# Toeplitz convolution in a recurrent block: eight products instead of ten in each middle block, with paired lags and paired inputs

## The reference, cut to what matters

```python
xn = layernorm(x)                                  # x: 2 x 1024 rows of 512
y = irfft(rfft(xn, n=1024) * rfft(K, n=1024))[..., :512]   # causal convolution along the 512 features
s = y + D[0] * xn                                  # K: 512 taps from a state-space model
h1, h3 = lora_linear(xn, w1), lora_linear(xn, w3)  # 512 -> 1376
g = silu(lora_linear(silu(h1) * h3, w2))           # 1376 -> 512
out = x + s * g
```

## Time and profile before

| what | value |
|---|---|
| median of 3 runs | 409.83 us (409.52 to 410.25) |
| the profiled execution: its time, its span | 409.98 us, 408.2 us |
| granted TensorE clock, mean | 0.999 |
| PE busy | 403.3 us (99% of the span), 1850 matmuls |
| DVE busy | 170.1 us (42%) |
| ACT busy | 105.9 us (26%) |
| POOL busy | 73.3 us (18%) |

### The profile page before, as it was taken

The page is one execution under the profiler, slowest core; times in us unless marked ns, Lnnn a source line. Parts: engine busy times, 40 slices in busy tenths (PEclk is TensorE's granted clock), DMA queues, the critical chain, the costliest instruction groups (busy, mean ns, idle before and its releaser), DMA issues.

```text
span 408.2 us, 5004 instructions
## 1 busy us (share of the span) xinstructions
PE 403.3 (99%) x1850; PEld 335.8 (82%) x1850; DVE 170.1 (42%) x267; ACT 105.9 (26%) x175; POOL 73.3 (18%) x139
## 2 busy tenths in 40 slices
PE   8999999999999999999999999999999999999996
PEld 8988888887788888888888888888888888888885
DVE  5887776794793322232343221233234111211125
ACT  7554232222351111221221111112222111111122
POOL 6685645402500114000000103300000000000000
PEclk9999999999999999999999999999999999999999
DMA  8573755604425101000016101000002000000002
GB/s 269 166 184 108 231 156 152 171 26 90 145 78 180 52 2 51 2 0 0 2 51 205 53 0 52 0 0 0 0 0 103 2 0 0 2 0 0 2 0 103
DMA packets 14466, 26.89 MB, mean 66 GB/s; under 512 B 2768, under 2 KB 4528, under 8 KB 14320
## 3 DMA queue, kind: packets, MB, share of 16 engines
q1 hardware_dynamic: 13440, 24.53, 19.2%
q0 software_dynamic: 720, 1.60, 2.0%
q10 hardware_dynamic: 288, 0.52, 0.3%
HBM read 21.45 MB, written 4.54 MB: 64 GB/s over the span
## 4 chain that ended last, share of the span: by engine, by line
PE 94%; DVE 3%; issue 1%; DMA 1%; ACT 1%; POOL 0%; DVEq 0%; POOLq 0%
PE h L991 20%; PE h L992 20%; PE h L993 20%; PE f L991 10%; PE f L992 10%; PE f L993 10%; PE h L1014 2%; PE spare L978 1%; DMA xn<-x_dram 1%; DVE raw L768 1%; PE spare L993 1%; PE spare L973 1%; PE spare L992 1%; PE spare L991 1%; DVE w L783 0%
## 5 line engine op out<-in xcount | busy, mean ns | idle before, releaser
L991 PE MATMUL h<-xt,w 128*128 (+2 forms) x340 | 131.4, 386 | 0.0
L992 PE MATMUL h<-xt,w 128*128 (+2 forms) x340 | 131.2, 386 | 0.0
L993 PE MATMUL h<-xt,w 128*128 (+2 forms) x340 | 131.2, 386 | 0.0
L991 PEld LDWEIGHTS h<-xt,w 128*128 128x128 f32 x340 | 63.9, 188 | 13.3 <-DVE w L780 0.4
L993 PEld LDWEIGHTS h<-xt,w 128*128 128x128 f32 x340 | 63.9, 188 | 12.9
L992 PEld LDWEIGHTS h<-xt,w 128*128 128x128 f32 x340 | 63.9, 188 | 12.3
L837 DVE TENSOR_TENSOR g<-g,h 128x512 f32<-128x512 f32 x40 | 27.5, 686 | 106.3 <-PE h L993 106.1
L842 DVE TENSOR_TENSOR ghl<-g,ghl 128x512 fp32r<-128x512 f32 x44 | 32.4, 736 | 90.0 <-ACT ghl L668 90.0
L991 PE MATMUL f<-ghl,w2f 128*128 128x512 f32 x176 | 68.8, 391 | 0.0
L992 PE MATMUL f<-ghl,w2f 128*128 128x512 f32 x176 | 68.6, 390 | 0.0
L993 PE MATMUL f<-ghl,w2f 128*128 128x512 f32 x176 | 68.5, 389 | 0.0
(11 more groups left out here) (141 smaller groups left out, 310.4 us busy)
## 6 DMA issues: line engine op xcount, KB each, us to landing
raw<-w_dram SPq DMA_DIRECT2D x28, 256.0 KB, 3.9
xres<-xT_dram SPq DMA_DIRECT2D x4, 1024.0 KB, 6.9
outT_dram<-xres SPq DMA_DIRECT2D x15, 256.0 KB, 2.5
rows_next<-x_dram SPq DMA_DIRECT2D x4, 512.0 KB, 3.6
scale_rows<-scales_scratch SPq DMA_DIRECT2D x3, 512.0 KB, 4.2
rows<-x_dram SPq DMA_DIRECT2D x2, 512.0 KB, 7.1
dft_sb<-dft_dram SPq DMA_DIRECT2D x1, 1024.0 KB, 5.0
raw<-w_dram SPq DMA_DIRECT2D x4, 224.0 KB, 3.2
```

The source lines that it names most:

```text
L991: pe.matmul(out, w[1], m[0], start=start, stop=False)
L992: pe.matmul(out, w[0], m[1], start=False, stop=False)
L993: return pe.matmul(out, w[0], m[0], start=False, stop=stop)
```

## The change

In blocks 1 and 2 the ten Toeplitz products become eight. Three use a sum of two inputs and a sum of two lags: with S(a,b) the product of such a pair, `(T0 + T1)(x0 + x1)` minus `T0 x0` and `T1 x1` gives `T1 x0 + T0 x1`, which is output chunk 1, and so on for the pairs (0, 2) and (1, 2). Blocks 0 and 3 keep their ten products.

- PE: `products` runs five of the eight behind `down` in tiles 2 (two products, T0 x0 and T1 x1, in the two spare banks), 4 (paired), 5 (T2 x2) and 6 (paired), all but the first two in the bank `spare1`. `last_product` runs the last three behind tile 10, and then `down` of tile 10 follows in one piece. The waits of the first gate and up part of a middle or last block become `conv_used` 1 and 2.
- DVE: `pair_sum` (three dependent additions for each pair, in tiles 4, 5 and 7 at "gate"), `pair_low` (the low part of the sum, in the same tiles at "up", behind `hidden_lo`), and `mix` (eight additions, subtractions and copies in all), which combines the products. `mid_sum` does what `out_sum` did.
- ACT: `pair_high` casts the high part of each pair's sum. `mid_gate` is `out_gate` with other buffers. Behind `out_gate` of block 0 ACT casts the high parts of the summed lags once.
- POOL: sums the lags once (T1 + T0 and T2 + T0 in one instruction of 256 columns, T1 + T2 in one of 128), behind `next_scale(1, 1)` of block 0, and subtracts the high parts when ACT has cast them. In the loop its wait for the convolution before `next_scale` is on `conv_used` instead of `conv_ready`.

The diff, without the new constants, addresses and semaphores that say nothing more:

```diff
--- before.py
+++ after.py
@@ -208,6 +208,16 @@
 K_PARTS = D // P
+MIX_AT = {(3, "gate"): (0,), (5, "gate"): (1,), (6, "gate"): (2,), (7, "gate"): (3,)}
+PAIRS = ((0, 1), (0, 2), (1, 2))
+PAIR_AT, PAIR_LO_AT = {(4, "gate"): 0, (5, "gate"): 1, (7, "gate"): 2}, {(4, "up"): 0, (5, "up"): 1, (7, "up"): 2}
+PRODUCTS_AT = {2: ((0, 0), (1, 1)), 4: ((0, 1),), 5: ((2, 2),), 6: ((0, 2),)}
+PRODUCTS = 5
 def spare_uses():
@@ -345,6 +365,12 @@
         gate = at("gate", [P, 2, BLK], lora_off + DC * BLK * 4)
         rows_next = at("rows_next", [P, 2, D], lora_off + (DC + 2) * BLK * 4)
         scale_rows = at("scale_rows", [P, 2, BLK], lora_off + (DC + 4) * BLK * 4)
+        pair_f = at("pair_whole", [P, BLK], lora_off + (DC + 3) * BLK * 4)
+        pair_lo = at("pair_lo", [P, BLK], lora_off + (DC + 3) * BLK * 4, F32R)
+        pair_hi = at("pair_hi", [P, BLK], tz_off, F32R)
+        y1, y2, less = gate[:, 0, :], gate[:, 1, :], rows_next[:, 0, :]
         assert lora_off + (DC + 6) * BLK * 4 <= xn_off
         rows_tile = 9
@@ -690,12 +719,28 @@
                         act.wait_ge(res_done, e - 1)
                     nc.scalar.activation(gate[:, n % 2, :], f[c][:, :], ACT.Silu).then_inc(gate_done, 1)
+            def pair_high(b, k):
+                act.wait_ge(pair_step, 9 * b - 9 + 3 * k + 3)
+                nc.scalar.copy(pair_hi[:, :], pair_f[:, :]).then_inc(pair_cast, 1)
+            def mid_gate(b):
+                for n, c in enumerate(OUT_ORDER):
+                    e = b * DC + n
+                    act.wait_ge(f_ready, e + 1)
+                    act.wait_ge(res_done, e - 1)
+                    nc.scalar.activation(scale_rows[:, n % 2, :], f[c][:, :], ACT.Silu).then_inc(gate_done, 1)
             def body(b, par_next, first, last):
+                mid = not first and not last
                 norm_at = NORM_AT_FIRST if first else NORM_AT
                 for j in range(HT):
                     for place in ("gate", "up", "down"):
                         if place == "gate" and not (first and j == 0):
                             hidden(b, j)
+                        if mid and (j, place) in PAIR_AT:
+                            if PAIR_AT[j, place] == 0:
+                                act.wait_ge(tsum_done, 2)
+                            pair_high(b, PAIR_AT[j, place])
                         if first:
                             for kind, t in folds(place, j):
                                 fold_hi(kind, t)
@@ -723,8 +768,13 @@
                     next_hi(b + 1, c, par_next)
                 if last:
                     last_gate(b)
+                elif mid:
+                    mid_gate(b)
                 else:
                     out_gate(b)
+                    act.wait_ge(tsum_added, 2)
+                    nc.scalar.copy(tsum[:, 0, :, :], tsum_f[:, :, :]).then_inc(tsum_hi, 1)
+                    nc.scalar.copy(t12_hi[:, :], t12_f[:, :]).then_inc(tsum_hi, 1)
             for r in (1, 2):
@@ -849,11 +899,65 @@
                 for i, (n, out, cols) in enumerate(steps):
                     part = gate_last(n)[:, cols]
                     dve.wait_ge(gate_done, b * DC + n + 1)
-                    dve.wait_ge(conv_ready, b * DC + i + 1)
+                    dve.wait_ge(conv_ready, DC + i + 1)
                     nc.vector.tensor_tensor(part, part, out[:, cols], ALU.mult).then_inc(conv_used, 1)
                     dve.wait_ge(conv_used, b * DC + i + 1)
                     sum_ = resid(par, LAST_ORDER[n])[:, cols]
                     nc.vector.tensor_tensor(sum_, sum_, part, ALU.add).then_inc(res_done, 1)
+            def pair_sum(b, par, k):
+                lo, hi = [[xt[:, par, hl, c, :].bitcast(F32) for c in PAIRS[k]] for hl in (1, 0)]
+                n = 9 * b - 9 + 3 * k
+                whole = pair_f[:, :]
+                nc.vector.tensor_tensor(whole, lo[0], lo[1], ALU.add).then_inc(pair_step, 1)
+                dve.wait_ge(pair_step, n + 1)
+                nc.vector.tensor_tensor(whole, whole, hi[0], ALU.add).then_inc(pair_step, 1)
+                dve.wait_ge(pair_step, n + 2)
+                nc.vector.tensor_tensor(whole, whole, hi[1], ALU.add).then_inc(pair_step, 1)
+            def pair_low(b, k):
+                dve.wait_ge(pair_cast, 3 * b - 3 + k + 1)
+                nc.vector.tensor_tensor(pair_lo[:, :], pair_f[:, :], pair_hi[:, :].bitcast(F32), ALU.subtract) \
+                    .then_inc(pair_ready, 1)
+            def mix(b, stage):
+                p, m, s = PRODUCTS * b - PRODUCTS, PRODUCTS * b - PRODUCTS, 3 * b - 3
+                dve.wait_ge(prod_ready, p + stage + 1)
+                if stage == 0:
+                    nc.vector.tensor_copy(y2, sp[1][:, :]).then_inc(mix_step, 1)
+                    dve.wait_ge(mix_step, s + 1)
+                    nc.vector.tensor_tensor(y1, sp[0][:, :], y2, ALU.add).then_inc(mix_done, 1)
+                if stage == 1:
+                    dve.wait_ge(mix_done, m + 1)
+                    nc.vector.tensor_tensor(y1, sp[1][:, :], y1, ALU.subtract).then_inc(mix_done, 1)
+                if stage == 2:
+                    nc.vector.tensor_tensor(less, y2, sp[1][:, :], ALU.add).then_inc(mix_step, 1)
+                    nc.vector.tensor_tensor(y2, y2, sp[1][:, :], ALU.subtract).then_inc(mix_done, 1)
+                    dve.wait_ge(mix_done, m + 3)
+                    nc.vector.tensor_tensor(y2, y2, sp[0][:, :], ALU.subtract).then_inc(mix_step, 1)
+                if stage == 3:
+                    dve.wait_ge(mix_step, s + 3)
+                    nc.vector.tensor_tensor(y2, y2, sp[1][:, :], ALU.add).then_inc(mix_done, 1)
+                if stage == 4:
+                    dve.wait_ge(mix_step, s + 3)
+                    nc.vector.tensor_tensor(less, sp[1][:, :], less, ALU.subtract).then_inc(mix_done, 1)
+            def mid_sum(b, par):
+                mix(b, 4)
+                dve.wait_ge(mix_done, PRODUCTS * b)
+                wait_residual(dve, b)
+                sums = {3: less, 2: y2, 1: y1, 0: sp[0][:, :]}
+                for n, c in enumerate(OUT_ORDER):
+                    e = b * DC + n
+                    part = scale_rows[:, n % 2, :]
+                    dve.wait_ge(gate_done, e + 1)
+                    nc.vector.tensor_tensor(part, part, sums[c], ALU.mult).then_inc(conv_used, 1)
+                    dve.wait_ge(conv_used, e + 1)
+                    if c < 2:
+                        dve.sem_inc(spare_free[c], 1)
+                    nc.vector.tensor_tensor(resid(par, c), resid(par, c), part, ALU.add).then_inc(res_done, 1)
             def out_sum(b, par):
                 for n, c in enumerate(OUT_ORDER):
@@ -873,9 +977,15 @@
                 norm_at = NORM_AT_FIRST if first else NORM_AT
                 split_at = SPLIT_AT_FIRST if first else SPLIT_AT
                 moments_at = MOMENTS_AT_FIRST if first else MOMENTS_AT
+                mid = not first and not last
                 late = []
                 for j in range(HT):
                     for place in ("gate", "up", "down"):
+                        if mid:
+                            for stage in MIX_AT.get((j, place), ()):
+                                mix(b, stage)
+                            if (j, place) in PAIR_AT:
+                                pair_sum(b, par, PAIR_AT[j, place])
                         if place == "up" and not (first and j == 0):
                             hidden_mul(b, j)
                         if first:
@@ -899,6 +1009,8 @@
                                     .then_inc(k_products, 1)
                         if place == "up":
                             hidden_lo(b, j)
+                        if mid and (j, place) in PAIR_LO_AT:
+                            pair_low(b, PAIR_LO_AT[j, place])
                         if first and (j, place) in RECIPROCAL_AT:
                             n = RECIPROCAL_AT.index((j, place))
                             dve.wait_ge(mag_ready, 1)
@@ -921,6 +1033,8 @@
                         next_lo(b + 1, c, par_next)
                 if last:
                     last_sum(b, par)
+                elif mid:
+                    mid_sum(b, par)
                 else:
                     out_sum(b, par)
@@ -1085,6 +1199,42 @@
                                [xt[:, par, hl, c, :] for hl in (0, 1)], c == 0, c == c_out)
                 mm.then_inc(conv_ready, 1)
+            def lag(d):
+                return [tzs[:, hl, d * P:(d + 1) * P] for hl in (0, 1)]
+            def single(b, par, d, out):
+                return three(out, lag(d), [xt[:, par, hl, d, :] for hl in (0, 1)], True, True)
+            def paired(b, k, out, start, stop):
+                pe.wait_ge(pair_ready, 3 * b - 3 + k + 1)
+                t = [t12_hi[:, :], t12_lo[:, :]] if k == 2 else [tsum[:, hl, k, :] for hl in (0, 1)]
+                return three(out, t, [pair_hi[:, :], pair_lo[:, :]], start, stop)
+            def products(b, par, j):
+                m = PRODUCTS * b - PRODUCTS
```

(57 more changed lines are left out.)

## The result

| | median, us | runs | ratio to before (95% interval) |
|---|---|---|---|
| before | 409.77 | 6 (409.47 to 410.68) | |
| after | 414.63 | 6 (414.01 to 416.38) | 1.0115 (1.0096 to 1.0134) |

The change makes the kernel slower by 4.9 us. 412.4 was forecast, with 413.7 as the upper end: the direction was right, and 2.2 us are missing. The profiled execution took 414.01, with a span of 412.2 (408.2 before) and a mean granted clock of 0.994 (0.999 before). The granted clock is the share of the full 2.4 GHz that TensorE was given.

The account below looks back on a forecast made before the run. PE, busy for 99% of the span, was taken as the bound. 409.98 (profiled) - 2.72 + 4.74 + 0.5 = 412.5, with the median 0.15 below the profiled run 412.4 us; range 411.2 to 413.7.

Parts of the forecast that it names:

- What is removed: Two products of three matmuls in two blocks, 12 matmuls at 0.2267 us each: 2.72 us less.
- The wait at the first paired product: Tile 4 of both middle blocks: PE stands still until DVE's pair_low, 2.37 us a block, 4.74 us in all.
- The start of block 1: Block 0 to block 1: POOL's two lag additions delay DVE and so the first matmul, 0.5 us, ends 0 and 1.0.
- The end of a middle block: Behind tile 10, down follows three products instead of four; 0.27 us of cover is left, cost 0.
- The other products, and the 20 instructions on DVE: Later products in the middle blocks have enough cover, and DVE's 20 added instructions a block fit its waits: cost 0.
- The clock: Rival, 3%: granted clock falls to the 1.2 GHz level after the tile 4 pause, 2.7 us a block, 417.8 us.
- POOL in between in tile 4: Rival, 10%: POOL's scaling runs before pair_low, some 1.1 us a block; 413.5 us for one, 414.6 for both.

Follow-up runs that it names:

- e3: The change with pair_low ahead of hidden_lo on DVE in tiles 4, 5 and 7, and POOL's lag additions ahead of its scaling: 407.12 us, ratio 0.9937.
- e1: The change with only pair_low put ahead of hidden_lo on DVE in tiles 4, 5 and 7 of the middle blocks: 407.61 us, ratio 0.9953.
- e2: The change with only POOL's two lag additions moved ahead of its scaling for block 1, the tile 4 stop kept: 413.63 us, ratio 1.0108.
- after_again: The changed kernel unaltered, run once more beside the kernels with more or less pause: 414.86 us, ratio 1.0131.
- e4: The change with nine more matmuls in tile 4 of each middle block, before the wait for the pair: 412.53 us, ratio 1.0071.
- e7: The change with three more matmuls in tile 4 of each middle block, before the wait for the pair: 412.47 us, ratio 1.0068.
- e5: The kernel before with one added PE wait behind down in tile 4 of each middle block, for the hidden tile's low part: 413.36 us, ratio 1.0090.
- e6: The kernel before with PE waiting in tile 4 of each middle block for one added DVE subtraction behind hidden_lo: 415.99 us, ratio 1.0163.

## Why the prediction was off, by its own steps

- **What is removed**, 2.72 us: right. e3 has hardly anything but this left and gains 2.58.
- **The wait at the first paired product**, 2.37 us a block: right in place, cause and size (2.30 and 2.31). PE resumed 0.16 after DVE's end (255.53 + 0.68 = 256.21; 256.60 - 0.2267 = 256.37), where 0.22 was taken. e1 shows the cause, since nothing but the order of two instructions differs.
- **The start of block 1**, 0.5 us: the cause is right, since e3 and e2, with the additions moved, have no gap, and between e1 and e3 it is 0.49. The size varies with the execution. The gap is 0.60 in the profile of the change, 0.30 in that of after_again, 0.49 in e1, 0.69 in e4 and 0.48 in e7, and against before the profile of the change is 0.31 late. That the wait at the end of block 0 could go away, as it did there, the prediction had not considered. The sizes by the line between two rows, 0.73 and 0.46, are what POOL took in e3, beside instructions of DVE that read only one operand from SBUF (L818, the other one comes from a matmul's bank).
- **The end of a middle block**, cover 0.27 us, cost 0: right. In block 1 `hidden_lo` of tile 10 ends at 211.35, and `down` follows the last product without a gap. The timelines, first DVE, then PE:

```profile
210.66 0.69 DVE L892 TENSOR_TENSOR ghl<-g,ghl 128x512 fp32r<-128x512 f32 x1 [1.26 <-ACT ghl L697]
```

```profile
211.64 0.39 PE L1107 MATMUL spare<-pair_hi,t_hi 128*128 128x512 f32 x1
211.87 0.40 PE L1105 MATMUL f<-ghl,w2f 128*128 128x512 f32 x1
```

- **The other products, and the 20 instructions on DVE:** cost 0, right (e1, e3).
- **The clock: this step failed.** The prediction kept it as a rival of 3%, since "the rows of 1.00 everywhere speak neither way", and left it out of the sum. The runs showed it in its place: all ten runs of the change have a mean clock of 0.990 to 0.996, none of e1, e3, e4, e5 and e7 is below 0.999, and the traces put the low stretch right behind a stop. Its price in the prediction, 2.7 us a block, was too high: the rows give 1.60 for each time, nine matmuls instead of twelve at the lower level, and those not wholly. 412.4 with one fall is 414.0, with two 415.6; the ten runs have 1.4 falls on average (six with one, four with two, by their clocks), which makes 414.6. Measured were 414.63 and 414.86.
- The fault was to read "no row shows it" as "unlikely". Once it has begun, PE waits for no more than 0.3 us at a time in the profile of before, so that its rows bore on neither answer, and the range should have reached over it on that side.
- **POOL in between in tile 4** did not happen: POOL's scaling starts at 256.78 in block 2, after `pair_low`. It does run beside `pair_sum` of tile 5, whose additions then take 1.65 and 1.55 us instead of 0.69, at no cost, as tile 5 covers them.

What stays open: why the clock falls behind one of two equal pauses and not behind the other. In the profiled run of the change it was block 2, in that of after_again block 1. Only stops of 1.6 to 1.7 us (e5, e7: no fall in 9 runs) and of 2.3 to 2.4 us (the change, e2, e6: a fall in 18 of 20 runs, by their mean clocks) were tried.

## What to carry to other kernels

Before new work is put into the queue of an in-order engine, ask what the instruction ahead of it waits for, and who asks for the new work: `pair_low` had 2 us of idle time ahead of `hidden_lo`, and stood behind it. A pause on TensorE costs more than its length if the clock falls behind it; count that as a case of its own wherever a change opens the first pause of this size. Here POOL's two small additions delayed DVE, and through it PE: put setup work where its engine idles and nobody depends on the pace of the engine beside it.

## What the runs showed of the hardware

- Three traces (after behind its second pause, after_again and e2 behind their first) show a pause of PE of 2.3 us followed, 1.0 to 1.5 us after PE had resumed, by 3.3 to 3.4 us at a granted clock of 0.51 to 0.52. The other pause in each of them, and both in the trace of e6, have a clock of 1.00 behind them. By mean clock and time, 18 of the 20 runs with two such pauses had at least one fall. With pauses of 1.6 to 1.7 us the mean clock stayed at 0.999 to 1.0 in 9 runs. In after_again PE had been without a gap for 39 us (118.50 to 157.50) ahead of the pause behind which the clock fell.

- The Trainium skill, page "SBUF — State Buffer", section "Who interferes with whom", has VectorE and GpSimd shut each other out for whole instructions when the VectorE instruction has two inputs in SBUF and the GpSimd instruction reads SBUF. The trace agrees as far as its sums go: POOL's addition of 256 columns took 1.18 us beside DVE's shift and split (L869, L873, two inputs in SBUF) and 0.73 in e3, and that of 128 columns 0.91 and 0.46. Which instruction waited for which isn't seen in the rows.
